# Attention over graph edges: transposed one-hots from broadcast node numbers, six banks, fetches first, and a lagged attention sum

## What is computed

```python
proj = x_norm @ Wp                       # [N, 8, 32]
score_s = (proj * a_src).sum(-1); score_t = (proj * a_trg).sum(-1)
e = exp(leaky_relu(score_s[s] + score_t[t], 0.2) - bound[t])
agg[t] = sum over edges of e * proj[s];  z[t] = sum over edges of e
x = x + elu(agg / (z + eps) + x_norm @ Wskip + bias)
```

## Time and profile before

| | us |
|---|---|
| runs | 8729.75 median of 3 (8719.02 to 8731.4) |
| the profiled execution | 8765.21 |
| its span | 8763.4 |
| attention loop, first gather to last accumulate | 1405.8 to 3845.8 |
| attention sum | 3855.9 to 4016.0 |

### The profile page before, as it was taken

One profiled execution on the slowest core, in us unless ns is written; L12 is line 12 of the kernel. 1 busy time (PEld: TensorE's weight loads), 2 busy tenths in 40 slices (PEclk: granted clock), 3 DMA queues, 4 the chain that ended last, 5 costly groups with the idle time before them and its releaser, 6 DMA issues. The chain is left out here.

```text
span 8763.4 us, 95624 instructions
## 1 busy us (share of the span) xinstructions
PE 6419.2 (73%) x28190; PEld 4535.2 (52%) x28190; DVE 5186.5 (59%) x11576; ACT 1653.8 (19%) x4694; POOL 3461.7 (40%) x3439
## 2 busy tenths in 40 slices
PE   5866665777777777744879778887888988852792
PEld 2444554556555555532454333444777777742561
DVE  7989886666666666665442266666655555562233
ACT  0322231111111111112222100000222122111220
POOL 0000003666666666620000155555665556534105
PEclk8987776777777777767989989999988888875896
DMA  2120001333333333320003322222222222222223
GB/s 71 43 74 6 1 1 53 92 91 92 92 91 91 92 92 90 92 54 16 0 21 128 126 68 70 69 72 74 84 81 80 77 78 80 80 46 89 72 63 103
DMA packets 294044, 612.38 MB, mean 70 GB/s; under 512 B 77333, under 2 KB 173443, under 8 KB 287078
## 3 DMA queue, kind: packets, MB, share of 16 engines
q0 software_dynamic: 180352, 455.22, 19.3%
q1 hardware_dynamic: 113231, 151.61, 5.1%
HBM read 494.20 MB, written 112.17 MB: 69 GB/s over the span
## 5 line engine op out<-in xcount | busy, mean ns | idle before, releaser
L1854 POOL DMA_INDIRECT ag_rows<-table,row_src x1612 | 1600.2, 993 | 2343.3 <-POOLq L939 1152.3
L1076 POOL DMA_INDIRECT at_rows<-table,row_dst x1612 | 1617.6, 1003 | 788.3 <-issue 437.8
L1210 PE MATMUL at_p_a<-at_rows,at_hot 128*125 128x264 f32 x3224 | 1289.5, 523 | 196.3 <-issue 165.4
L1161 DVE TENSOR_TENSOR acc<-acc,at_p_a 125x264 f32 x1612 | 687.2, 426 | 871.7 <-DMA a_row<-in_L_gnn_a_trg 614.4
L1210 PEld LDWEIGHTS at_p_a<-at_rows,at_hot 128*125 128x125 f32 x3224 | 738.1, 260 | 471.8 <-issue 311.4
L2214 PE MATMUL mo_p_e<-ag_rows,ag_hot 128*125 128x256 f32 x2192 | 679.2, 437 | 279.5 <-DVE acc L2059 222.0
L2059 DVE TENSOR_TENSOR acc<-acc,mo_p_e 125x256 f32 x1096 | 459.3, 419 | 617.0 <-PE mo_p_e L2214 340.1
L1177 PE MATMUL at_p_t<-ident,at_hot 128*125 128x128 f32 x1612 | 430.4, 362 | 410.7 <-ACT at_hot_t L1086 360.7
L2214 PEld LDWEIGHTS mo_p_e<-ag_rows,ag_hot 128*125 128x125 f32 x2192 | 409.1, 207 | 497.0 <-DVE acc L2059 356.4
L1177 PEld LDWEIGHTS at_p_t<-ident,at_hot 128*125 128x125 f32 x1612 | 335.0, 256 | 535.3 <-issue 460.6
L1963 DVE TENSOR_TENSOR mo_prod<-mo_far,mo_twice 125x256 f32<-125x256 f32 x1600 | 580.1, 419 | 50.5 <-issue 43.9
(11 more groups left out here) (445 smaller groups left out, 10008.6 us busy)
## 6 DMA issues: line engine op xcount, KB each, us to landing
table<-rt_row SPq DMA_DIRECT2D x50, 1000.0 KB
at_rows<-table,row_dst POOLq DMA_INDIRECT x1612
ag_rows<-table,row_src POOLq DMA_INDIRECT x1612
moe_in<-ones SPq DMA_DIRECT2D x1, 13440.0 KB
ex_space<-moe_in SPq DMA_DIRECT2D x105, 128.0 KB, 2.2
moe_out<-ex_space SPq DMA_DIRECT2D x105, 128.0 KB, 1.7
table<-row SPq DMA_DIRECT2D x50, 128.9 KB
x<-in_x SPq DMA_DIRECT2D x1, 6250.0 KB
```

Of the source, the lines that this page charges most:

```text
L1076: pool.indirect_dma_start(out=rows[n % 3][:, g, :], out_offset=None, in_=m.table0, in_offset=bass.IndirectOffsetOnAxis(ap=row_i[:, n * G + ...
L1161: dve.tensor_tensor(row, row, p_a[g % 4][0:P, 0:TW], ALU.add).then_inc(s_acc, 1)
L1210: pe.matmul(p_a[g % 4][0:P, 0:TW], hot[v][:, g, :], rows[v][:, g, :], start=True, stop=True).then_inc(s_agg, 1)
L1854: pool.indirect_dma_start(out=rows[:, i % RING, j, :], out_offset=None, in_=m.table1, in_offset=bass.IndirectOffsetOnAxis(ap=row_i[:, 2 * ...
```

## The change

- PE's transposes and ScalarE's copies of them go. The second sort also writes its node numbers, in edge order and as bf16, to a DRAM buffer `node_t` (four VectorE operations and one DMA of 0.5 MB). In the loop SyncE broadcasts the 1664 numbers of a step to all 125 partitions, into two buffers, and ScalarE makes the transposed one-hots with two activations: Abs(number - partition), then Relu(1 - that).
- The two PSUM banks that are free now go to the aggregation, which has six.
- PE's order in a step is `fetch(n + 2)` first, then the 13 aggregation tiles.
- VectorE loads the step's tile numbers at the top of the step, ahead of its wait for the fetch, and no longer behind the first two scalings.
- ScalarE's order in a step is Exp, distances, scores, one-hots, for step n + 3.
- The bias is added to the skip rows in `sorts_and_rows`, by a matmul of one row, and no longer in `attention_add`.
- `attention_add` is unrolled and lagged: the product of tile n is issued while Exp of tile n - 1 runs; it has four skip buffers.

```diff
--- attend
+        wide = [sb(f"at_wide{u}", [P, G * 128], BF16) for u in range(2)]
+        dist = sb("at_dist", [P, G * 128], BF16)
+        minus_p = sb("at_minus_p", [P, 1], F32)
-        p_t = [ps(f"at_p_t{k}", [128, 512]) for k in range(2)]
-        p_a = [ps(f"at_p_a{k}", [128, 512]) for k in range(4)]
+        p_a = [ps(f"at_p_a{k}", [128, 512]) for k in range(BANKS)]
...
+            @block.sync
+            def _(sp):
+                for n in range(NG):
+                    if n >= 2:
+                        sp.wait_ge(s_dist, n - 1)
+                    sp.dma_start(wide[n % 2][:, :], m.node_t[n * G * 128:(n + 1) * G * 128]
+                                 .rearrange("(o e) -> o e", o=1).broadcast_to((P, G * 128))).then_inc(s_wide[n % 2], 16)
...
+                def distance(n):
+                    act.wait_ge(s_wide[n % 2], 16 * (n // 2) + 16)
+                    if n >= 1:
+                        act.wait_ge(s_hot_t, n)
+                    act.activation(dist[:, :], wide[n % 2][:, :], ACT.Abs, bias=minus_p[:, 0:1]).then_inc(s_dist, 1)
+
+                def one_hot_turned(n):
+                    act.wait_ge(s_dist, n + 1)
+                    if n >= 1:
+                        act.wait_ge(s_fetch, n)
+                    act.activation(hot_t[:, :, :].rearrange("p g e -> p (g e)"), dist[:, :], ACT.Relu, bias=m.ones[0:P, 0:1],
+                                   scale=-1.0).then_inc(s_hot_t, 1)
...
+                for n in range(3):
+                    distance(n)
+                    score_rows(n, n % 2)
+                    one_hot_turned(n)
+
+                for n in range(NG):
                     act.wait_ge(s_diff, n + 1)
+                    act.activation(rows[n % 3][:, :, C:TW], diff[:, :, :], ACT.Exp).then_inc(s_exp, 1)
+                    if n + 3 < NG:
+                        distance(n + 3)
+                        score_rows(n + 3, (n + 3) % 2)
+                        one_hot_turned(n + 3)
...
                 def step(n, w, lap):
                     u, v = w % 2, w % 3
                     f = p_f[u][:, 0:2 * H * G].rearrange("p (g s) -> p g s", g=G)
+                    tiles = tiles_of(nc, mybir.EngineType.DVE, m.tile_dst, n)
                     dve.wait_ge(s_fetch, n + 1)
...
                     scale_rows(0)
                     scale_rows(1)
-                    tiles = tiles_of(nc, mybir.EngineType.DVE, m.tile_dst, n)
...
                 def fetch(n, u):
 
-                    pe.wait_ge(s_hot_t, n * NQ + NQ)
+                    pe.wait_ge(s_hot_t, n + 1)
                     pe.wait_ge(s_near, n * G + G)
-                    if later(n):
+                    if n >= 2:
                         pe.wait_ge(s_diff, n - 1)
...
+                fetch(0, 0)
+                fetch(1, 1)
+                for n in range(NG):
+                    if n + 2 < NG:
+                        fetch(n + 2, n % 2)
                     for g in range(G):
+                        k = n * G + g
                         if g % 4 == 0:
+                            pe.wait_ge(s_hot, n * NQ + g // 4 + 1)
                             pe.wait_ge(s_msg, n * NQ + g // 4 + 1)
+                        if k >= BANKS:
+                            pe.wait_ge(s_acc, k - BANKS + 1)
+                        pe.matmul(p_a[k % BANKS][0:P, 0:TW], hot[n % 3][:, g, :], rows[n % 3][:, g, :],
                                   start=True, stop=True).then_inc(s_agg, 1)
--- sorts_and_rows, vector, end of the second sort
+                        if s == 1:
+                            half = FS // 2
+                            low, high = keys[0][:, 0:half], keys[0][:, half:FS].bitcast(BF16)
+                            for h in range(2):
+                                dve.tensor_scalar(bits(low), bits(buf[at][:, half * h:half * h + half]), shift, LANES - 1,
+                                                  ALU.logical_shift_right, ALU.bitwise_and)
+                                dve.drain()
+                                dve.tensor_copy(high[:, half * h:half * h + half], bits(low))
+                                dve.drain()
+                            dve.drain().then_inc(s_node_t, 1)
--- sorts_and_rows, tensor
+                        pe.matmul(p_a[0:P, C:2 * C], m.ones[0:1, 0:P], skip_b[:, :], start=False, stop=False)
--- attention_add, vector
+                for n in range(NT + 1):
+                    u, e = n % 2, n - 1
+                    if n < NT:
+                        dve.tensor_tensor(y[u][:, :].rearrange("p (h f) -> p h f", h=H),
+                                          acc[:, n, 0:C].rearrange("p (h f) -> p h f", h=H),
+                                          z[:, n, :].unsqueeze(2).broadcast_to((P, H, D)), ALU.mult)
+                    if n >= 1:
+                        dve.wait_ge(s_exp, e + 1)
+                        dve.scalar_tensor_tensor(out=y[1 - u][:, :], in0=y[1 - u][:, :], scalar=0.0, in1=low[1 - u][:, :],
+                                                 op0=ALU.max, op1=ALU.add)
                     dve.drain()
+                    if n < NT:
+                        dve.wait_ge(s_skip[n % 4], 16 * (n // 4 + 1))
+                        dve.tensor_tensor(y[u][:, :], y[u][:, :], skip[n % 4][:, :], ALU.add).then_inc(s_sum, 1)
+                    if n >= 1:
+                        dve.scalar_tensor_tensor(out=m.x[:, e, :], in0=y[1 - u][:, :], scalar=-1.0, in1=m.x[:, e, :],
+                                                 op0=ALU.add, op1=ALU.add)
+                    if n < NT:
+                        dve.drain()
+                        dve.tensor_scalar(low[u][:, :], y[u][:, :], 0.0, None, ALU.min).then_inc(s_low, 1)
```

More of the change, by code:

```diff
@@ L39 @@
 DS = 64
+BANKS = 6
 class Shared:
@@ L856, in row_work @@
                             pe.wait_ge(s_act, n)
-                        for c in range(2):
-                            mm = pe.matmul(p_a[0:P, :], xnt[:, c, n * P:n * P + P], w_ps[:, c, :], start=c == 0, stop=c == 1)
-                        mm.then_inc(s_ma, 1)
+                        pe.matmul(p_a[0:P, :], xnt[:, 0, n * P:n * P + P], w_ps[:, 0, :], start=True, stop=False)
+                        pe.matmul(p_a[0:P, C:2 * C], m.ones[0:1, 0:P], skip_b[:, :], start=False, stop=False)
+                        pe.matmul(p_a[0:P, :], xnt[:, 1, n * P:n * P + P], w_ps[:, 1, :], start=False, stop=True
+                                  ).then_inc(s_ma, 1)
                         yield
@@ L1160, in step @@
                         row = acc[:, bass.ds(tiles[g], 1), :].rearrange("p o w -> p (o w)")
[L1161 removed]
+                        dve.tensor_tensor(row, row, p_a[(n * G + g) % BANKS][0:P, 0:TW], ALU.add).then_inc(s_acc, 1)
                         if g in (1, 3):
@@ L1190, in fetch @@
                     mm.then_inc(s_fetch, 1)
-                for n in range(2):
-                    for g in range(G):
-                        turn(n, n, g)
-                    fetch(n, n)
-                def step(n, w, lap):
-                    u, v = w % 2, w % 3
-                    ahead = not (isinstance(n, int) and n + 2 >= NG)
-                    if ahead:
-                        for g in range(8):
-                            turn(n + 2, (w + 2) % 3, g)
-                    for g in range(G):
+                fetch(0, 0)
[3 more added lines that the diff above has]
+                        fetch(n + 2, n % 2)
+                    for g in range(G):
+                        k = n * G + g
                         if g % 4 == 0:
+                            pe.wait_ge(s_hot, n * NQ + g // 4 + 1)
                             pe.wait_ge(s_msg, n * NQ + g // 4 + 1)
-                        if g >= 4:
-                            pe.wait_ge(s_acc, n * G + g - 3)
-                        elif g == 0 and not (isinstance(n, int) and n == 0):
-                            pe.wait_ge(s_acc, n * G)
-                        pe.matmul(p_a[g % 4][0:P, 0:TW], hot[v][:, g, :], rows[v][:, g, :],
-                                  start=True, stop=True).then_inc(s_agg, 1)
-                        if ahead and 3 <= g < 3 + G - 8:
-                            turn(n + 2, (w + 2) % 3, g + 5)
-                    if ahead:
-                        fetch(n + 2, u)
-                in_rings(pe, step)
+                        if k >= BANKS:
+                            pe.wait_ge(s_acc, k - BANKS + 1)
+                        pe.matmul(p_a[k % BANKS][0:P, 0:TW], hot[n % 3][:, g, :], rows[n % 3][:, g, :],
+                                  start=True, stop=True).then_inc(s_agg, 1)
 def attention_sums(nc, m, acc, smax, z):
@@ L1254, in attention_add @@
         sb, ps, sem = m.scope(nc, ctx)
-        bias = sb("aa_bias", [P, C], F32)
-        skip = [sb(f"aa_skip{u}", [P, C], F32) for u in range(2)]
+        skip = [sb(f"aa_skip{u}", [P, C], F32) for u in range(4)]
         y = [sb(f"aa_y{u}", [P, C], F32) for u in range(2)]
         low = [sb(f"aa_low{u}", [P, C], F32) for u in range(2)]
```

(14 more changed lines are left out.)

76 lines of the change are left out of this document (18 added, 58 removed).

## The result

| | before | after |
|---|---|---|
| median of the runs | 8724.39 us (8713.01 to 8731.4) | 8876.12 us (8855.85 to 8895.99) |
| profiled execution: time, span | 8765.2, 8763.4 us | 8874.88, 8873.0 us |

A forecast was written before the change was run, and what follows sets the result against it. The attention loop was taken as bound by 13 gathers plus late-told PE completions, 19.4 us a step. Terms +190 - 5 - 54 + 3 = +134 us gave 8899 profiled, 8864 for the runs, range 8670 to 8965.

The forecast's parts named there:

- The new cycle: Attention loop: the step grows by 1.6 us to 21.0 us, +190 us over 121 steps.
- the new hold: Attention loop: release 3.2 us after the last gather, VectorE starting 8.2 us after a difference, still ending last.
- the hold: Attention loop: what PE has finished is told late to waiting engines, until 3.2 us after the last gather.
- Fetch at 0.50 because PE is idle: Attention loop: the fetch's 26 matmuls, behind PE's idle time, take 5.7 us at clock 0.50; lower end 3.0.
- The load and the fetch's place are the cost: Attention loop: fetch moved ahead of the aggregation takes 5.7 us; VectorE's register load at the step's top adds 2.1.
- The hold belongs to the stream of gathers: Attention loop: late-told PE completions come with a long unbroken gather stream, absent in its first 8 us.
- Two ScalarE activations, 0: Attention loop: one-hots by two activations of 1.6 us each cost 0, since ScalarE is mostly idle.
- Broadcast, 0: Attention loop: broadcasting node numbers, 0.42 MB a step under the gathers, costs 0, at most +1 us a step.
- Loop start, -5: Start of the attention loop: one link less in the waits of PE and ScalarE, -5 us, bounds 0 and -25.
- Bias matmuls, 0, bounded by 20: Row stage: fifty one-row matmuls on PE cost 0 because VectorE sets the pace; up to 20 us without that cover.
- Sum, -54: Attention sum: lagged tiles take 2.12 us each, 108 us for 160, in all -54 us; bounds -35 and -62.
- Sort's end, +3: End of the sort: four VectorE operations on 1024 columns, 0.65 us each, with three drains, +3 us.

The follow-up runs named there:

- the filler: Changed kernel without bias matmuls, plus 24 unread matmuls a step in PE's idle time and five aggregation banks: 8293.16 us, ratio 1.0102, on the chip without late releases.
- the lagged sum alone: Kernel before with only the lagged attention sum, PE writing skip + bias to PSUM: 8679.07 us, ratio 0.9967.
- the seven gathers: Kernel before with 7 of 13 gathers by GpSimd, same bytes by plain DMA: 8123.45 us (0.9331) with late releases, 7898.21 us (0.9617) on the chip without.
- the first candidate: Changed kernel with fetch last, register load back, partition numbers early, bias added by GpSimd in the sum: 8197.11 us, ratio 0.9971, on the chip without late releases.

## Why the prediction was right, and where it was not

- *The new cycle* (+190): +159. Its steps came as listed: the fetch took 5.70 us at 0.50 (forecast 5.7), the first tile was through 6.9 us after the difference (7.1), the load showed with 2.07 us (2.1). The term that was too large is *the new hold*: it was released 2.3 us behind the last gather, not 3.2, so VectorE started at 7.63 and not 8.2. The gathers restarted at 9.35 us (10.0) and took 16.3 (15.7). That the hold still ends last is right by 0.5 us only: the chain had become almost as long, and the fast chip's step without any hold is 0.36 us shorter.
- *Fetch at 0.50 because PE is idle*: the filler shows that without the idle time the fetch runs at 1.00. It gives no rule: in the lagged sum alone, PE was busy throughout and the clock stayed at 0.50. The row that I took the clock from ends at 2606.10, where the gap begins, so the 0.50 had begun 4.8 us ahead of it. And half of 9.76 is 4.9 us, not 5.5; PE's idle time came as forecast all the same (6.72). *The load and the fetch's place are the cost*: shown; with the fetch last the step is 19.0, and the load is then free in the mean.
- *The hold belongs to the stream of gathers*: the seven gathers bear it out on a chip that has it, with their number as a rival to the length of the stream. That every chip has it was assumed without a word, and is wrong.
- *Two ScalarE activations, 0*: 1.67 and 1.68 us (1.6), no table load for Abs or Relu. This agrees with the Trainium skill, page "ScalarE: Activation LUTs", section "Table sets: the hidden batching unit", which has such functions in every set. The rule in section "Rules for kernel authors" of the same page of the Trainium skill, to give relu to VectorE, would by these rows have made things worse: VectorE is in the chain, and ScalarE waits 11.4 us ahead of an Exp. No run tried it.
- *Broadcast, 0*: its start meets a gather that takes 1.99 us in place of 0.95, once a step. This lengthens the time to the last gather and so the hold, but the step by no more than the 0.36 us that the hold is worth. No run takes the broadcast out.
- *Loop start, -5*: wrong, +16.3. "One link less" overlooked that ScalarE makes three sets of one-hots ahead of the first Exp, the third behind a held fetch, and that an iota stands ahead of the first gather. Without the iota the start was 6.1 us shorter; with two sets and the fetch last it was 5.5 and 8.2 us shorter in the two runs that have that. If these add up, 2 to 5 of the 16.3 us are left open.
- *Bias matmuls, 0, bounded by 20*: wrong, 24. VectorE, 203 of 219 us busy, looked like the pace of the row tiles; PE, 178 of 219, shared it in a ring. Neither was full, so each tile's own order PE, ScalarE, VectorE, PE may set the period; that ring is my reading. What is shown is that the 0.48 us added to each of 50 tiles came through. The bound of 0.4 us was also too low: a bias matmul is two overlapping records of 0.43 us, 0.69 us together.
- *Sum, -54*: -51.0. *Sort's end, +3*: the four operations take from 1398.92 to 1401.92. Some 2.5 of the 29.7 us ahead of the loop are in none of my terms.

The start came out 21 us and the bias 24 us dearer than forecast, the loop 31 cheaper: so 8864 was nearer to 8876 than its terms were to theirs. That the misses cancel is luck; that the loop sets the sign and most of the size is not.

## What to carry to other kernels

Where an engine waits for another that is told of late, find out what releases it before giving its slack away: here 5.3 us of slack on VectorE were free to use only as long as the fetch ran behind the accumulates. A step of PE that is moved in front of the chain is paid at the clock that it gets there (5.70 us at 0.50 here, 3.04 at 1.00), and a register load is free only where its engine waits anyway. Before a matmul is called hidden behind a busier engine, see whether any engine is really full (203 of 219 us was not), and price it as if it weren't hidden.

## What the runs showed that I had not expected

- With 13 gathers a step, PE's completions were told late on the chips where the kernel before takes about 8715 us, as far as they were profiled (a release 2.3 to 3.2 us behind the last gather), and on time on the one where it takes 8212, even with an unbroken stream (0.81 us). The change costs far more on that chip: without the bias matmuls, and so without 24 us of its cost, it takes 8584.44 us there against 8211.9, 373 us more; on the other chips the whole change costs 152. If the kernel before is bound by its gathers there as the first candidate was, 3.4 us a step (20.3 less 16.9) account for it; there is no profile of that kernel there. What differs between the chips stays open.
- GpSimd's first instruction of another kind is late: the iota starts 12.85 us behind the instruction before it, and the first addition in the first candidate's sum kept VectorE waiting 10.3 us (of which the skip rows' DMA may be 2.9). Both follow a reduction over all partitions; a gather behind the same reduction starts after 2.32 us. The Trainium skill, page "GPSIMD Engine Reference", section "2.1 Instruction dispatch", has about 6 us for the first call of a freshly loaded kernel; the rows show more, and the rows decide; whether this is the same thing was not tried.
